# The order of values, denominators and key/value products in a fused gated attention and expert kernel

## The chip, the cores and the metric

The kernel runs on one core of one Trainium2 chip. Its time is the device time of one launch in microseconds (us). The core has TensorE (PE in the rows; PEld are its weight loads), VectorE (DVE), ScalarE (ACT), GpSimd (POOL) and SyncE (SP, which issues the transfers). They run their own instruction streams in order and meet through semaphores.

## What is computed

The reference is a gated cross attention followed by a gated layer of experts, in float32:

```python
x = x + tanh(g_xattn) * xattn(layernorm(x), ctx)        # x: 4 x 512 x 256, ctx: 4 x 1024 x 256
x = x + tanh(g_ffn) * ffn(layernorm(x))

# xattn, 16 heads of 64
lat, ctx = layer_norm(latents), layer_norm(context)
q = lat @ Wq                                            # 256 -> 1024
k, v = split(ctx @ Wkv)                                 # 256 -> 2 x 1024
k = rope(k, cos, sin)                                   # x1*cos - x2*sin, x2*cos + x1*sin
attn = softmax(clip(q k^T / 8, -11, 11))
out = (attn v) @ Wo + bo

# ffn: 4 experts of width 1024, each row goes to 2 of them, exact gelu
```

## The kernel before

**Stages.** A start (to about 45 us) loads and transposes the first batch, then the attention runs over 128 steps (to about 870 us), then come the routed experts. A batch has four units of four heads, a unit has eight steps (s = 0 to 7), and its two halves are pairs of heads (p), with c = s % 4 as the step within a pair. i = u * 8 + s counts the steps of a batch, 0 to 31. The loop over the batches in the program holds units 1, 2, 3 and the next batch's unit 0; the last three units are written out apart, with `last` true.

**One step.** It works on two context tiles of 128 rows for one pair:
- TensorE, `score`: the scores of the two tiles, twelve matmuls (L1519) into the banks `sc0` and `sc1`. Products that need float32 accuracy are made of three matmuls of a high and a low part.
- ScalarE, `exps`: exponential of each bank into `prob` (L800), 128 x 1024 each. `prob` has two halves by the step's parity.
- VectorE, `clamp`: the clip, as a clamp of the exponentials (L1004), for each bank; `sums`: adds them into `acc` (L1016 for c = 1, L1019 for c = 2 and 3; nothing for c = 0).
- TensorE, `values`: attention times values for the *preceding* step, eight matmuls into `pv` (L1533). They wait for that step's clamps (`clamped`).
- TensorE, `kv_make`: keys and values of tile s of the *next* unit, six matmuls into the bank `kv` (L1464 to L1466). They wait until VectorE has read that bank for the tile before (`rot1`).
- The key's rotation: ScalarE copies key and value out of `kv` (`kv_evac`, L748 and L749); GpSimd multiplies by the sines (L610); VectorE multiplies by the cosines from `kv` (`rot_cos`, L993); GpSimd adds the two (L614, semaphore `rot`).
- TensorE, `k_turn`: transposes the rotated key of the tile *before* this step's (L1505) into the bank `tr`. It waits for `rot` and `k_ready`. ScalarE rounds it to the high part (`k_split`, L742), VectorE makes the low part (`k_low`, L957, semaphore `k_ready`), which also frees `tr`.

**Once in a pair.** In its first step (c = 0), `denominators` (L1543, into the bank `mi`) sums `acc` of the pair before over the partitions, and waits for both last sums; VectorE then makes `reciprocals` (L1024, L1028, L1032). In the second step (c = 1) VectorE's `normalise` (L1038) reads `pv` first of all, and `values`, which begin a new accumulation in `pv` there, wait for it; `q_make` makes the next pair's query. For s = 2 and 3 `project` multiplies by the output weights and `residual` adds the product on VectorE.

**The steps that turn.** The next batch's context is normalised and transposed beside this work: for i = 18 to 25 a step ends with `ctx_turn` (L1471), for i = 26 and 27 with `lat_turn` (L1478), both into `tr`, and so both wait for `k_ready` of this step's key. ScalarE's `ctx_affine` (L758, four pieces) reads them and stands ahead of the next step's exponentials; VectorE's `ctx_low` (L943) makes their low part one step later. For i = 19 to 28 (`turned`) `kv_make` stands ahead of `k_turn`, since the bank `tr` is longer in use. In the last batch the router's rows are turned in the same way for i = 10 to 15 (`x_turn`), with `turned` for i = 11 to 16. Just ahead of the turning, GpSimd's `lat_scale` (L590 to L596) makes the latents' scale in i = 15, behind the output weights' low part (L604).

**What sets the order.** No scheduler: each engine's `step` function writes its instructions out, and the engine takes them in that order. All four `step` functions are called with the same (b, u, s). The change touches those of VectorE and of TensorE.

## Time and profile before

| | us |
|---|---|
| median of 3 runs | 1193.79 |
| lowest and highest | 1192.82 to 1195.61 |
| profiled execution | 1203.28 |
| its span, first to last instruction | 1201.5 |
| TensorE busy | 1123.1 (93%) |
| VectorE busy | 1026.8 (85%) |
| ScalarE busy | 649.5 (54%) |
| GpSimd busy | 617.9 (51%) |

The busy times are of the profiled execution. A busy TensorE is not a TensorE at its peak, since matmuls overlap and their ends are modelled: the distance from start to start of two groups tells what one costs. The TensorE clock that was granted is 0.987 of full speed over the span. In the rows a wait stands in brackets behind an instruction: the engine's idle time just before it, and what ended it.

### The profile page before, as it was taken

To read this page: it belongs to the slowest core of one execution; us is meant where nothing else is said; L and a number is where in the kernel's file an instruction comes from. 1 tells how busy PE (TensorE), PEld (TensorE's weight loads), DVE (VectorE), ACT (ScalarE), POOL (GpSimd) and SP (SyncE) were. 2 spreads that over 40 slices of the span, in tenths; PEclk is the share of its full clock that TensorE was granted. 3 is DMA by queue.
4 is the path that set the end of the run, shared out by engine and by line. 5 is a ranking of instruction groups with operands and counts; after the bars stand their busy time and mean duration, and the time that the engine had idled before them with its cause. 6 is when DMAs were issued, how large, how long until landed. Compare 5 with 4: busy or idle time off the path is not lost.

```text
span 1201.5 us, 22865 instructions
## 1 busy us (share of the span) xinstructions
PE 1123.1 (93%) x8087; PEld 758.0 (63%) x8087; DVE 1026.8 (85%) x1751; ACT 649.5 (54%) x1223; POOL 617.9 (51%) x593
## 2 busy tenths in 40 slices
PE   5799999999999999999999999997789989999987
PEld 3555555555555555465555556653379989999777
DVE  6699999898899998989999998889678777775886
ACT  4555566655456665455666455534456666663321
POOL 5333565343356535335644343238558767885750
PEclk9999999999999999999999999999999999999989
DMA  6000100000000000000000022002347555665102
GB/s 176 32 10 15 31 23 14 10 10 20 19 19 28 10 10 10 21 19 19 28 10 10 18 79 72 10 23 102 123 136 242 194 172 179 204 218 176 51 29 70
DMA packets 67080, 79.33 MB, mean 66 GB/s; under 512 B 10888, under 2 KB 60432, under 8 KB 66960
## 3 DMA queue, kind: packets, MB, share of 16 engines
q1 hardware_dynamic: 64640, 71.47, 18.5%
q0 software_dynamic: 2304, 6.29, 1.6%
q8 instruction: 70, 1.15, 0.4%
q14 instruction: 50, 0.41, 0.1%
q10 hardware_dynamic: 16, 0.00, 0.0%
HBM read 64.65 MB, written 13.11 MB: 65 GB/s over the span
## 4 chain that ended last, share of the span: by engine, by line
PE 68%; DVE 15%; POOL 6%; issue 6%; ACT 2%; DMA 1%; SPq 1%; another core or an unknown queue 0%; POOLq 0%; DVEq 0%; ACTq 0%
PE pv L1533 14%; PE sc L1519 12%; PE kv L1464 5%; PE kv L1466 4%; PE kv L1465 4%; PE sc L1464 4%; PE sc L1466 4%; PE sc L1465 4%; PE tr L1505 3%; DVE acc L1019 3%; PE mi L1464 3%; PE mi L1465 3%; PE mi L1466 3%; POOL slots_x L639 2%; PE mi L1543 2%
## 5 line engine op out<-in xcount | busy, mean ns | idle before, releaser
L800 ACT ACTIVATE prob<-sc 128x1024 f32<-128x1024 f32 x256 | 249.6, 1028 | 217.8 <-PE sc L1519 210.6
L610 POOL TENSOR_TENSOR rot_s<-k_raw,sinb 128x256 f32<-128x256 f32 x128 | 108.7, 850 | 389.3 <-ACT k_raw L748 389.3
L1533 PE MATMUL pv<-prob,val 128*32 128x512 f32 x2048 | 245.7, 597 | 3.0 <-DVE recip L1038 1.8
L1519 PE MATMUL sc<-q_hid,big 64*128 64x512 f32 x1536 | 214.7, 411 | 10.1 <-ACT prob L800 6.4
L1004 DVE TENSOR_SCALAR prob<-prob 128x1024 f32<-128x1024 f32 x256 | 183.8, 731 | 44.5 <-ACT prob L800 40.3
L1519 PEld LDWEIGHTS sc<-q_hid,big 64*128 64x128 f32 x1536 | 135.8, 186 | 115.0 <-issue 68.4
L1019 DVE TENSOR_TENSOR acc<-acc,prob 128x1024 f32<-128x1024 f32 x128 | 195.6, 1549 | 0.0
L614 POOL TENSOR_TENSOR rot_c<-rot_c,rot_s 128x256 f32<-128x256 f32 x128 | 122.0, 953 | 42.0 <-DVE rot_c L993 27.0
L1533 PEld LDWEIGHTS pv<-prob,val 128*32 128x32 f32 x2048 | 56.6, 109 | 111.9 <-issue 90.8
L1464 PE MATMUL kv<-big,acts 128*128 128x512 f32 x256 | 114.5, 447 | 6.2 <-DVE rot_c L993 5.0
L659 POOL TENSOR_TENSOR big<-prob,big 128x512 fp32r<-128x512 f32 x72 | 92.6, 1294 | 49.0 <-ACT big L827 45.2
L659 POOL TENSOR_TENSOR big<-val,big 128x512 fp32r<-128x512 f32 x72 | 93.1, 1300 | 27.6 <-ACT big L827 23.1
L1466 PE MATMUL kv<-big,acts 128*128 128x512 f32 x256 | 102.4, 400 | 0.0
L1465 PE MATMUL kv<-big,acts 128*128 128x512 f32 x256 | 102.1, 399 | 0.0
L1464 PE MATMUL sc<-big,q_hid 128*128 128x256 f32 x304 | 89.5, 295 | 10.5 <-DVE q_hid L1374 10.0
L1016 DVE TENSOR_TENSOR acc<-prob 128x1024 f32<-128x1024 f32 x64 | 93.7, 1503 | 0.0
L1465 PE MATMUL sc<-big,q_hid 128*128 128x256 f32 x304 | 87.1, 287 | 1.1 <-issue 1.1
L1466 PE MATMUL sc<-big,q_hid 128*128 128x256 f32 x304 | 87.2, 287 | 0.0
L748 ACT ACTIVATE k_raw<-kv 128x256 f32<-128x256 f32 x128 | 50.1, 391 | 62.5 <-PE kv L1466 59.9
L993 DVE TENSOR_TENSOR rot_c<-kv,cosb 128x256 f32<-128x256 f32 x128 | 53.8, 420 | 34.7 <-ACT val L749 30.5
L1464 PEld LDWEIGHTS sc<-big,q_hid 128*128 128x128 f32 x304 | 59.3, 195 | 13.5 <-DVE q_hid L1374 12.4
L1505 PE MATMUL tr<-ident,rot_c 128*128 128x128 f32 x256 | 54.3, 294 | 12.9 <-POOL rot_c L614 12.9
(250 smaller groups left out, 2515.3 us busy)
## 6 DMA issues: line engine op xcount, KB each, us to landing
val<-in_L_ffn_w SPq DMA_DIRECT2D x18, 1024.0 KB, 5.6
prob<-in_L_ffn_w SPq DMA_DIRECT2D x18, 1024.0 KB, 5.6
rows<-in_ctx SPq DMA_DIRECT2D x32, 128.0 KB, 2.1
w_raw<-in_L_xattn_Wq SPq DMA_DIRECT2D x16, 256.0 KB, 2.6
w_raw<-in_L_xattn_Wo SPq DMA_DIRECT2D x64, 64.0 KB
slots_x<-c_aff SPq DMA_DIRECT2D x1, 3840.0 KB, 13.1
rows<-slots_x SPq DMA_DIRECT2D x15, 256.0 KB, 7.9
slots_y<-acc SPq DMA_DIRECT2D x15, 256.0 KB, 2.1
```

The lines of the kernel that those rows point to most:

```text
L610: g.tensor_tensor(rot_s[:].rearrange("p (h a c) -> p h a c", h=4, a=2), kh[:, :, ::-1, :], sinb[:, t].unsqueeze(1).to_broadcast([P, 4, 2, ...
L614: g.tensor_tensor(k_rot[:], rot_c[:], rot_s[:], ALU.add).then_inc(rot, 1)
L659: low = g.tensor_tensor(w_of(job, half, 1)[:, cols], raw_of(job, half)[:, cols], w_of(job, half, 0)[:, cols].bitcast(F32), ALU.subtract)
L800: a.activation(prob[:, s % 2, i, :], sc[i][:], ACT.Exp, scale=DH ** -0.5).then_inc(exp_done[i], 1)
L1004: v.tensor_scalar(prob[:, s % 2, i, :], prob[:, s % 2, i, :], EXP_LOW, EXP_HIGH, ALU.max, ALU.min).then_inc(clamped[i], 1)
L1016: v.tensor_tensor(acc[:, i, :], prob[:, 0, i, :], prob[:, 1, i, :], ALU.add).then_inc(summed[i], 1)
L1019: v.tensor_tensor(acc[:, i, :], acc[:, i, :], prob[:, s % 2, i, :], ALU.add).then_inc(summed[i], 1)
L1464: mm(dst, lhs(0), rhs(0), start=start, stop=False, **kw)
L1465: mm(dst, lhs(0), rhs(1), start=False, stop=False, **kw)
L1466: return mm(dst, lhs(1), rhs(0), start=False, stop=stop, **kw)
L1519: last = mm(sc[i][:, h * N:(h + 1) * N], kst[rows_h, u % 2, j, lk, t * P:(t + 1) * P], q_sp[rows_h, p % 2, lq, :], start=lk + lq == 0, sto ...
L1533: last = mm(pv[g * 32:(g + 1) * 32, :], val[:, u % 2, 2 * c + i, at:at + 32], prob[:, s % 2, i, h * N:(h + 1) * N], start=c == 0 and i == ...
```

## The change

On TensorE, in every step of the attention:
- `values` of the preceding step come directly behind the scores, where c is not 1. Where c is 1 they stay last of the group, behind key transpose, key/value product, output product and query.
- `denominators` follow the values, ahead of key transpose and key/value product.
- So the key/value product ends the plain step, or is followed only by the output product. Where `turned` is true it stands ahead of the key transpose as before, and the transpose is then followed directly by the context's or the latents'.

On VectorE, the first of the two sums comes directly behind the clamps, ahead of `rot_cos` and `k_low`; the context's and the latents' low parts move ahead of it, so that they are still made before it. The second sum stays behind.

```diff
@@ VectorE, step
                 clamp(b, u, s, 1)
+                if not last and 0 <= i - TURN - 1 < ST:
+                    ctx_low(b + 1, i - TURN - 1)
+                if not last and 0 <= i - L_TURN - 1 < 2:
+                    lat_low(b + 1, i - L_TURN - 1)
+                sums(b, u, s, 0)
                 if make:
                     rot_cos(*next_unit(b, u), s)
                 if s == 0:
...
                 if last and i == R_RANK + 2:
                     route_slots()
-                if not last and 0 <= i - TURN - 1 < ST:
-                    ctx_low(b + 1, i - TURN - 1)
-                if not last and 0 <= i - L_TURN - 1 < 2:
-                    lat_low(b + 1, i - L_TURN - 1)
-                sums(b, u, s, 0)
@@ TensorE, step
                 score(b, u, s, 1)
+                if c != 1 and not (is_first(b, u) and s == 0):
+                    values(*((b, u, s - 1) if s else (b, u - 1, STEPS - 1) if u else (b - 1, UNITS - 1, STEPS - 1)))
+                if c == 0 and not (is_first(b, u) and s == 0):
+
+                    pe.wait_ge(q_ready, pair_no(b, p) + 1)
+                    wait(pe, wo_out, (b * UNITS + u) * 2 - (2 if s == 0 else 0))
+                    denominators(*((b, p - 1) if p else (b - 1, PAIRS - 1)))
                 turned = not last and 0 <= i - TURN - 1 < ST + 2 or last and R_TURN < i <= R_TURN + EH
                 if make and turned:
                     kv_make(nb, nu, s)
...
                 if make and not turned:
                     kv_make(nb, nu, s)
-                if c == 0 and not (is_first(b, u) and s == 0):
-
-                    pe.wait_ge(q_ready, pair_no(b, p) + 1)
-                    wait(pe, wo_out, (b * UNITS + u) * 2 - (2 if s == 0 else 0))
-                    denominators(*((b, p - 1) if p else (b - 1, PAIRS - 1)))
...
-                if not (is_first(b, u) and s == 0):
+                if c == 1:
                     values(*((b, u, s - 1) if s else (b, u - 1, STEPS - 1) if u else (b - 1, UNITS - 1, STEPS - 1)))
```

TensorE, from a pair's first step (its key/value product, L1464 to L1466) into its second, before. `kv`, `mi`, `pv`, `sc` and `tr` are the banks written: key/value, denominators, values, scores, key transpose.

```order
 L1465 MATMUL kv<-big,acts 128x512
 L1466 MATMUL kv<-big,acts 128x512
 L1543 MATMUL mi<-acc,ones 32x256 x8
 L1533 MATMUL pv<-prob,val 32x512 x8
 L1519 MATMUL sc<-q_hid,big 128x512 x12
 L1505 MATMUL tr<-ident,rot_c 128x128 x2
```

The same place with the change:

```order
 L1465 MATMUL kv<-big,acts 128x512
 L1466 MATMUL kv<-big,acts 128x512
 L1519 MATMUL sc<-q_hid,big 128x512 x12
 L1505 MATMUL tr<-ident,rot_c 128x128 x2
 L1464 MATMUL kv<-big,acts 128x512
```

Between a key/value product and the transpose of its key (L1505), denominators and values are gone, and the scores alone are left.

TensorE, the end of a step that turns (i = 22, c = 2), before:

```order
 L1465 MATMUL kv<-big,acts 128x512
 L1466 MATMUL kv<-big,acts 128x512
 L1505 MATMUL tr<-ident,rot_c 128x128 x2
 L1533 MATMUL pv<-prob,val 32x512 x8
 L1469 REGISTER_ALU
 L1471 MATMUL tr<-ident,rows 128x128 x2
```

and with the change:

```order
 L1465 MATMUL kv<-big,acts 128x512
 L1466 MATMUL kv<-big,acts 128x512
 L1505 MATMUL tr<-ident,rot_c 128x128 x2
 L1469 REGISTER_ALU
 L1471 MATMUL tr<-ident,rows 128x128 x2
 L1519 MATMUL sc<-q_hid,big 128x512 x12
```

The values no longer stand between the key transpose and the context transpose (L1471), which write the same bank.

VectorE, a step that turns (L1004 clamps, L943 context's low half, L1019 sums, L993 and L957 the key's rotation and low half), before:

```order
 L1004 TENSOR_SCALAR prob<-prob 128x1024
 L992 REGISTER_ALU
 L993 TENSOR_TENSOR rot_c<-kv,cosb 128x256
 L957 TENSOR_TENSOR big<-tr,big 128x2x128
 L943 TENSOR_TENSOR acts<-c_aff,acts 128x2x128
 L1018 ISA
 L1019 TENSOR_TENSOR acc<-acc,prob 128x1024 x2
```

and with the change:

```order
 L1004 TENSOR_SCALAR prob<-prob 128x1024
 L943 TENSOR_TENSOR acts<-c_aff,acts 128x2x128
 L1018 ISA
 L1019 TENSOR_TENSOR acc<-acc,prob 128x1024
 L992 REGISTER_ALU
 L993 TENSOR_TENSOR rot_c<-kv,cosb 128x256
 L957 TENSOR_TENSOR big<-tr,big 128x2x128
 L1019 TENSOR_TENSOR acc<-acc,prob 128x1024
```

The context's low half and one sum have moved ahead of the key's rotation and of its low half, which frees the bank `tr`.

## Rows read from the trace of the kernel before

**Rows 1.** Busy times, 75 to 760 us: PE, PEld, DVE, ACT, POOL, clock, DMA
```profile
75.00:760.00 685.00, 673.38 (x4835) 385.73 (x4834) 630.79 (x1046) 391.51 (x737) 309.41 (x310) 1.00 0.07 22
```

**Rows 2.** In order of time, a bare step on TensorE (start, length, engine, line)
```profile
646.86 1.67 PE L1519 MATMUL sc<-q_hid,big 64*128 64x512 f32 x12
...
648.46 0.44 PE L1505 MATMUL tr<-ident,rot_c 128*128 128x128 f32 x2
...
650.22 1.92 PE L1533 MATMUL pv<-prob,val 128*32 128x512 f32 x16
...
652.08 1.65 PE L1519 MATMUL sc<-q_hid,big 64*128 64x512 f32 x12
```

**Rows 3.** In order of time, TensorE, VectorE and GpSimd, the attention's first step
```profile
44.74 0.40 PE L1466 MATMUL kv<-big,acts 128*128 128x512 f32 x1
...
45.29 1.67 PE L1519 MATMUL sc<-q_hid,big 64*128 64x512 f32 x12
...
45.94 0.42 DVE L993 TENSOR_TENSOR rot_c<-kv,cosb 128x256 f32<-128x256 f32 x1 [2.24 <-ACT val L749]
...
46.28 0.41 DVE L957 TENSOR_TENSOR big<-tr,big 128x256 fp32r<-128x256 f32 x1
...
46.88 0.72 POOL L614 TENSOR_TENSOR rot_c<-rot_c,rot_s 128x256 f32<-128x256 f32 x1 [0.51 <-POOL rot_s L610]
...
47.66 0.44 PE L1505 MATMUL tr<-ident,rot_c 128*128 128x128 f32 x2 [0.70 <-POOL rot_c L614]
```

**Rows 4.** In order of time, TensorE alone, context transposes of one batch
```profile
572.81 0.44 PE L1471 MATMUL tr<-ident,rows 128*128 128x128 f32 x2
...
593.35 0.44 PE L1471 MATMUL tr<-ident,rows 128*128 128x128 f32 x2
...
599.17 0.43 PE L1471 MATMUL tr<-ident,rows 128*128 128x128 f32 x2
...
605.41 0.43 PE L1471 MATMUL tr<-ident,rows 128*128 128x128 f32 x2 [0.56 <-DVE big L957]
...
612.28 0.43 PE L1471 MATMUL tr<-ident,rows 128*128 128x128 f32 x2 [0.33 <-DVE big L957]
...
619.29 0.44 PE L1471 MATMUL tr<-ident,rows 128*128 128x128 f32 x2
```

**Rows 5.** In order of time, ScalarE and TensorE, the step from 605.77 us
```profile
606.13 0.81 ACT L758 ACTIVATE acts<-tr,affine 128x128 fp32r<-128x128 f32 x2 [1.82 <-DVE acts L943]
...
607.51 1.94 ACT L800 ACTIVATE prob<-sc 128x1024 f32<-128x1024 f32 x2
...
609.17 1.07 PE L1543 MATMUL mi<-acc,ones 128*32 128x256 f32 x16
...
610.05 1.90 PE L1533 MATMUL pv<-prob,val 128*32 128x512 f32 x16
```

**Rows 6.** In order of time, GpSimd and TensorE, step i = 17 of a batch
```profile
552.23 2.28 POOL L604 TENSOR_TENSOR wo<-w_raw,wo 128x512 fp32r<-128x512 f32 x1
...
560.92 0.44 PE L1505 MATMUL tr<-ident,rot_c 128*128 128x128 f32 x2 [1.24 <-POOL rot_c L614]
```

**Rows 7.** In order of time, TensorE and VectorE, a pair's reciprocals
```profile
663.35 1.66 PE L1519 MATMUL sc<-q_hid,big 64*128 64x512 f32 x12
...
663.57 0.43 DVE L1024 STREAM_TRANSPOSE recip<-mi 128x256 f32<-128x256 f32 x1
...
664.04 0.83 DVE L1028 RECIPROCAL rc<-recip 64x8 f32<-64x8 f32 x4
...
664.91 0.71 DVE L1032 STREAM_TRANSPOSE recip<-rc 128x512 f32<-128x512 f32 x1
```

**Rows 8.** Groups by line (busy us, mean ns of one, idle before them)
```profile
L1019 DVE TENSOR_TENSOR acc<-acc,prob 128x1024 f32<-128x1024 f32 x128 | 195.6, 1549 | 0.0
...
L1004 DVE TENSOR_SCALAR prob<-prob 128x1024 f32<-128x1024 f32 x256 | 183.8, 731 | 44.5 <-ACT prob L800 40.3 <-issue 0.8 <-DVE gate L1302 0.2
```

**Rows 9.** In order of time, GpSimd, a rotation beside a softmax sum
```profile
656.96 1.76 POOL L614 TENSOR_TENSOR rot_c<-rot_c,rot_s 128x256 f32<-128x256 f32 x1
```

## The prediction

> **What bounds the kernel now.** I read four views in this order. First the busy time by stretches: between 75 and 760 us, where the attention runs at full pace, TensorE is busy 673.38 of 685 us at a granted clock of 1.00 and VectorE 630.79 us [rows 1]. So TensorE sets the time there, with 11.6 us of idle time in all, and VectorE is close behind. Second the instructions in order of time in a bare step (one with no denominators, no query or output product): scores, key transpose, key/value product and values follow each other without a hole. From 646.86 to 652.08 that is 5.22 us: 1.60 for the scores (to 648.46), 1.76 for transpose and product (to 650.22), 1.86 for the values [rows 2]. Third the same view of TensorE's context transposes (L1471), whose distances give the lengths of the steps that also turn the next batch's context [rows 4]. Fourth the waits with VectorE at the end of them in those steps [rows 5]. Since TensorE is nearly full, whatever makes it wait anew adds to the time, and a gain can't exceed those 11.6 us by much: I look for what each new place in the order waits for.
>
> The Trainium skill (Perfetto Trace Analysis, Identifying the Most-Contended Engine) says that matmul busy time is no good measure of how near TensorE is to its limit, and to look at the weight loads, here 385.73 of 685 us [rows 1]. By that one would see room on TensorE, and the sum below would shrink towards nothing. The start-to-start distances of a bare step, without a gap between groups [rows 2], decide against it.
>
> **Part 1, the order on TensorE in plain steps.** The products are the same; only who stands behind whom changes. Before, a key/value product was followed by values (1.86) and scores (1.60) before its key was transposed. Now, where c is not 1, it is followed by scores and values: the same 3.46 us, so the rotation on ScalarE, GpSimd and VectorE stays hidden. Costed at nothing. In a pair's second step (c = 1) only the scores stand between: 1.60 us. What the rotation needs, the start of the attention shows, where no values exist yet and the order is exactly this one: the product's last matmul starts at 44.74 and ends at 45.14, VectorE's half starts at 45.94, GpSimd's sum at 46.88, the transpose at 47.66, after 0.70 us of idle TensorE [rows 3]. That wait is the least the order can cost with the engines otherwise idle; I take 0.65, as an estimate that lets the two engines overlap slightly better than there (bounds 0.55, and 0.9 for a VectorE that is late). Steps of this kind with a key/value product ahead, not turning, and not already in this order: 22. That is 14.3 us.
>
> **Part 2, the same place behind GpSimd's long chain.** In step i = 17 of each of the first three batches the transpose already waits 1.24 us, because GpSimd works from 552.23 on the output weights and the latents' scale before it can rotate; the transpose comes at 560.92 [rows 6], 8.69 us later. The chain starts when the rotation of step i = 15 is done, and that step's product now stands behind the values instead of ahead of them, 1.86 us later. The chain and the transpose behind it slip by about 1.9 us; 0.65 is counted already, so 1.25 more, three times: 3.8 us (bounds 0 and 6).
>
> **Part 3, the denominators.** They stay about 3.4 us into a pair's first step, now behind the values. They wait for the last sum. VectorE reaches the pair's second step later: in the first step its rotation waits for a product that is now last, so the transposes and reciprocals (0.43 + 0.83 + 0.71, from 663.57 to 665.62 [rows 7]) start when the key's low half is written, some 1.5 us after the step's end, where 663.57 was 0.2 us behind the end at 663.35. That is 1.3 us later at VectorE, against 0.7 us by which the next pair's denominators come later (0.65 of part 1 and 0.1 of order). Only where bare steps leave VectorE little slack (a unit's end, 10 times) can the rest surface: 0.4 us each, 4 us; bounds 0 and 1.2 each.
>
> **Part 4, the steps that turn.** Ten steps of each of the first three batches (i = 19 to 28) put the key/value product ahead of the key transpose, and nine end with a context or latent transpose into the same bank. It must wait until VectorE has read the key out of that bank. Before, the values (1.86) stood between and covered this. Now only c = 1 keeps them there. After a product's end the key's low half is written 1.55 us later at best (46.28 + 0.41 against 45.14 [rows 3]). And VectorE now does its first sum (mean 1.549 us [rows 8]) between the clamps and the rotation, which closes a loop: context transpose 0.43, ScalarE starts 0.05 later, its four affine pieces 1.4 (606.13 to 607.51), two exponentials 1.94, last clamp 0.73, context's low half 0.34, first sum 1.55, rotation 0.34 and key's low half 0.41, and again the transpose: 7.26 us [rows 5, 8]. (0.34 is the start-to-start distance of two such operations in rows 3.)
> - A pair's last step: 7.26.
> - A pair's first step has no sum, but scores 1.60, values 1.86, denominators 0.88 (609.17 to 610.05), product 1.6 and 1.6 for rotation and low half, with 0.4 for the transpose: 7.9.
> - Second step: the reciprocals and normalisation (0.43 + 0.83 + 0.71 [rows 7], and the product with `pv`) take longer than ScalarE's part of the loop; an estimate of 0.25: 7.5.
> - Third step: the query's rounding stands ahead of the exponentials; I estimate it at 0.6, between an affine piece of 0.35 and an exponential of 0.97 [rows 5]: 7.85.
>
> Now against what rows 4 give: i = 19 to 21 took 20.54 together and become 7.26 + 7.9 + 7.5 = 22.66 (+2.1); i = 22, 5.82 to 7.85 (+2.0); i = 23, 6.24 to 7.26 (+1.0); i = 24, 6.87 to 7.9 (+1.0); i = 25, 7.01 to 7.5 (+0.5). For i = 26 and 27, which have an output product behind the key transpose and so more cover, I take half of what i = 22 and 23 lose, +1.5 together. That is 8.1 a batch, 24.3 for three. The lower bound leaves the loop out and keeps only the 1.6 us behind the product in steps without an output product: 4 a batch, 12. The upper takes GpSimd beside VectorE, below: 12 a batch, 36.
>
> In the last batch six steps turn the router's rows in the same manner, with fewer waits behind them; I take 2 us in all, bounds 0 and 5. Later steps of that batch wait for routing work that nothing here moves: nothing.
>
> **GpSimd beside VectorE.** A rotation sum takes 0.72 us alone [rows 3] and 1.76 us beside a softmax sum [rows 9]. The first sum now lies where GpSimd multiplies k by the sines. In plain steps there are 3.46 us of cover, against the 2.5 of rows 3, so 1.0 more is just hidden; I take nothing for it, and put it in the upper bounds. The Trainium skill (SBUF — State Buffer, Who interferes with whom) says that a VectorE instruction with two SBUF inputs and a GpSimd instruction that reads SBUF exclude each other for a whole instruction. The 1.76 us agrees. By that rule both of GpSimd's operations would stand behind a sum, and the third rival below would be the case; the sum here does not lean on it.
>
> **Sum.** 14.3 + 3.8 + 4 + 24.3 + 2 = 48.4 us. The profiled execution took 1203.28 us, with a span of 1201.5, so it would become 1251.7. The median of the runs without a profile is 1193.79, 9.5 us less; I add the same 48.4 to it: **1242.2 us**. By the lower bounds: 12.1 + 0 + 0 + 12 + 0 = 24; by the upper: 20 + 6 + 12 + 36 + 5 = 79.
>
> **The rivals.**
> - *The turning steps stay covered.* VectorE and ScalarE start each step earlier than I think, since the values no longer stand before the transposes, and the loop hides; only parts 1 to 3 remain: 1193.8 + 22 = 1216. For it: VectorE waits little in those steps now (0.33 us at 612.28 is TensorE's wait for it, not the reverse [rows 4]). Against: the 1.6 us behind the product need no busy VectorE.
> - *Faster.* The sum fills the hole in which VectorE waits for the value copy, so it keeps ahead of TensorE, and the 11.6 us of idle go in part: VectorE's lateness ends the idle time in front of the context transposes (0.56 and 0.33 us [rows 4]). It decides if the key's rotation fits behind the scores, that is in under 1.60 us from the product's end; then parts 1 and 4 vanish and about 8 us are gained: 1186. Against it: rows 3 show 2.5 us.
> - *GpSimd falls behind in every step.* Each key transpose of the other steps waits too, by 0.4 us in about 70 steps (the 1.0 us more of rows 9 on two operations, less the cover): 28 on top, 1270.
> - *The order doesn't bite.* Semaphores other than the order set the pace, and the time stays: 1194. Against: the order on TensorE is fixed in the program, and the engine is full.
>
> **How the numbers follow.** Forecast 0.64; turning steps covered 0.14; GpSimd behind 0.12; faster 0.07; unchanged 0.03. The range leaves out the faster and the unchanged case and the far end of the third: 1212 to 1272. A measurement of this kernel can tell about 0.2% (2.4 us) from no change. Faster by more 0.07, within 0.03, slower 0.90.
>
> **What would show it.** Right: TensorE's key transposes (L1505) wait for GpSimd's L614 in every second step of a pair, by 0.55 to 0.9 us; its context transposes (L1471) wait for VectorE's L957 by 1 to 2 us; a bare plain step stays at 5.2 us; the idle time between 75 us and the attention's end grows from 11.6 to about 58 us; the expert stage behind it keeps its length. Wrong, and how: if L1471 shows no new wait, part 4 falls; if L1505 waits in steps with c = 2 and 3 too, the third rival holds; if the denominators (L1543) wait over 1 us, part 3 was too small.

## The result, and the profile with the change

The changed kernel takes 1248.64 us, median of 4 runs (1247.43 to 1251.06), against 1193.3 us for the kernel before (4 runs, 1191.22 to 1195.61). The ratio is 1.0471, with a 95% interval of 1.0446 to 1.0497. It is slower by 55.3 us. The prediction was 1242.2, within 1212 to 1272.

The profiled execution took 1247.43 us, with a span of 1245.7. The attention of the last batch now ends some 55 us later, so I read 75 to 815 us where [rows 1] have 75 to 760. The columns are those of [rows 1]:

```profile
75.00:815.00 740.00, 685.62 (x4868) 392.94 (x4864) 622.82 (x1057) 396.79 (x743) 292.92 (x314) 0.99 0.07 20
```

TensorE is idle for 54.4 us (740.00 - 685.62) where it was idle for 11.6. The mean clock fell from 1.00 to 0.99, which looks like nothing and is not. The two longest sums of waits in the same stretch, TensorE only (sum in us, how often, longest):

```profile
PE tr L1505 <- POOL rot_c L614: 24.8, 23, 2.8
PE tr L1471 <- DVE big L957: 19.6, 21, 1.6
```

Before, the same two stood at 6.6 and 2.6 us over 75 to 815 us (4.1 and 2.6 over 75 to 760 us, which holds about the same steps):

```profile
PE tr L1505 <- POOL rot_c L614: 6.6, 6, 1.5
...
PE tr L1471 <- DVE big L957: 2.6, 6, 0.6
```

Two kinds of wait were foreseen and both came. Where they lie is seen best by the length of each step, from the start of its scores (L1519) to the start of the next one's. Subtracting the two kernels step by step, up to step 124 of 128, gives 54.99 us, nearly the 55.3 us of the medians. A second profile of the kernel before, below, is 2.7 us later at that step, so this is known to about 3 us. By kind of step (us, the changed kernel minus the kernel before, from one profile of each):

| steps | how many | predicted | measured |
|---|---|---|---|
| plain second steps, c = 1 | 17 | 0.65 each | +9.6, 0.56 each |
| i = 17 | 3 | 1.9 each | +9.3, 3.1 each |
| i = 15 | 3 | 0 | +7.1, 2.4 each |
| turning, i = 19 to 27 | 27 | +24.3 | +18.8 |
| the last batch, i = 8 to 16, with its turning steps | 9 | +2 | +5.2 |
| all other steps up to there | 54 | +4 | +1.3 |
| start, and the attention's end | 11 | 0 | +3.7 |

The first row holds one step that had the changed order already (the attention's second) and kept its length. The other 16 lost 0.60 us each. A 17th of this kind, i = 9 of the last batch (+0.6), is in the fifth row, together with i = 8 (-0.8, at the end of the program's loop); i = 10 to 16 alone are +5.3.

**A plain second step** (i = 13 of the second batch), TensorE, VectorE and GpSimd in order of time. The product's last matmul is followed by the scores alone, and the transpose waits 0.57 us. The rotation's pieces are those of [rows 3], at nearly the same distances:

```profile
346.38 0.40 PE L1466 MATMUL kv<-big,acts 128*128 128x512 f32 x1
346.70 1.66 PE L1519 MATMUL sc<-q_hid,big 64*128 64x512 f32 x12
...
347.27 0.74 POOL L610 TENSOR_TENSOR rot_s<-k_raw,sinb 128x256 f32<-128x256 f32 x1 [4.63 <-ACT k_raw L748]
...
347.50 0.43 DVE L993 TENSOR_TENSOR rot_c<-kv,cosb 128x256 f32<-128x256 f32 x1 [1.95 <-ACT val L749]
...
348.15 0.73 POOL L614 TENSOR_TENSOR rot_c<-rot_c,rot_s 128x256 f32<-128x256 f32 x1
...
348.94 0.44 PE L1505 MATMUL tr<-ident,rot_c 128*128 128x128 f32 x2 [0.57 <-POOL rot_c L614]
```

**A turning step** (i = 22 of the third batch). It now lasts from 634.33 to 641.61, 7.28 us, where it lasted 5.8. The last product matmul ends at 639.44, VectorE's first sum stands ahead of the rotation, and the context transpose waits 1.59 us for the key's low half:

```profile
639.05 0.39 PE L1466 MATMUL kv<-big,acts 128*128 128x512 f32 x1
639.24 1.22 DVE L1019 TENSOR_TENSOR acc<-acc,prob 128x1024 f32<-128x1024 f32 x1
...
640.38 0.42 DVE L993 TENSOR_TENSOR rot_c<-kv,cosb 128x256 f32<-128x256 f32 x1
640.71 0.41 DVE L957 TENSOR_TENSOR big<-tr,big 128x256 fp32r<-128x256 f32 x1
641.04 1.21 DVE L1019 TENSOR_TENSOR acc<-acc,prob 128x1024 f32<-128x1024 f32 x1
...
641.25 0.43 PE L1471 MATMUL tr<-ident,rows 128*128 128x128 f32 x2 [1.59 <-DVE big L957]
641.61 1.20 PE L1519 MATMUL sc<-q_hid,big 64*128 64x512 f32 x8
```

**Step i = 15** was a bare step of 5.20 us and now takes 7.57, in all three batches. I had not foreseen this one. VectorE and GpSimd, with the transpose that waits:

```profile
581.68 1.20 DVE L1019 TENSOR_TENSOR acc<-acc,prob 128x1024 f32<-128x1024 f32 x1
581.83 3.97 POOL L614 TENSOR_TENSOR rot_c<-rot_c,rot_s 128x256 f32<-128x256 f32 x1
...
582.81 1.28 DVE L1004 TENSOR_SCALAR prob<-prob 128x1024 f32<-128x1024 f32 x2
584.01 1.21 DVE L1019 TENSOR_TENSOR acc<-acc,prob 128x1024 f32<-128x1024 f32 x1
...
585.86 0.44 PE L1505 MATMUL tr<-ident,rot_c 128*128 128x128 f32 x2 [2.31 <-POOL rot_c L614]
```

GpSimd's addition, 0.72 us alone [rows 3] and 1.76 us beside one sum [rows 9], takes 3.97 us. It starts 0.15 us behind the start of one sum and ends (585.80) 0.58 us behind the end of the next (585.22). VectorE runs sum, clamp, clamp, sum there, four instructions without a gap.

**Step i = 17** waits as in [rows 6], but 2.78 instead of 1.24 us, and then something else happens:

```profile
590.86 1.75 POOL L604 TENSOR_TENSOR wo<-w_raw,wo 128x512 fp32r<-128x512 f32 x1
...
598.13 0.44 PE L1505 MATMUL tr<-ident,rot_c 128*128 128x128 f32 x2 [2.78 <-POOL rot_c L614]
...
598.64 0.39 PE L1465 MATMUL kv<-big,acts 128*128 128x512 f32 x1
...
599.59 0.63 PE L1465 MATMUL kv<-big,acts 128*128 128x512 f32 x1
```

The same matmul goes from 0.39 to 0.63 us. TensorE and its clock in two stretches there (us, TensorE busy, granted clock, transfers' share and rate):

```profile
600.00:602.50 2.50, 2.50 (x7) 0.51 0.01 3
602.80:604.60 1.80, 1.80 (x17) 1.00 0.00 0
```

After the wait the clock was granted at the lower of its two levels (1.2 GHz) for some 3 us, and step i = 17 is longer by 1.54 us of wait and about 1.56 us of slow matmuls.

### The profile page after: what moved, and what is told of

Read it like the earlier page. It is cut to its first block, busy times and chain, and to the rows that moved or that the text cites. A ratio compares the mean times of both kernels' runs of the same rounds, so it can differ in the third digit from the quotient of the medians.

```text
span 1245.7 us, 22865 instructions
## 1 busy us (share of the span) xinstructions
PE 1128.9 (91%) x8087; PEld 759.3 (61%) x8087; DVE 1001.3 (80%) x1751; ACT 652.6 (52%) x1223; POOL 599.7 (48%) x593
## 4 chain that ended last, share of the span: by engine, by line
PE 61%; DVE 16%; issue 8%; POOL 8%; ACT 6%; DMA 1%; SPq 0%; POOLq 0%; DVEq 0%; ACTq 0%
PE pv L1533 13%; PE sc L1519 9%; PE kv L1464 5%; PE kv L1466 4%; PE kv L1465 4%; PE sc L1464 4%; PE sc L1466 4%; PE sc L1465 4%; PE tr L1505 2%; POOL rot_c L614 2%; DVE acc L1016 2%; ACT prob L800 2%; POOL rot_s L610 2%; POOL slots_x L639 2%; PE mi L1543 2%
## 5 line engine op out<-in xcount | busy, mean ns | idle before, releaser
L610 POOL TENSOR_TENSOR rot_s<-k_raw,sinb 128x256 f32<-128x256 f32 x128 | 112.2, 877 | 437.0 <-ACT k_raw L748 436.9
L1533 PE MATMUL pv<-prob,val 128*32 128x512 f32 x2048 | 248.3, 603 | 4.2 <-DVE recip L1038 3.0
L1004 DVE TENSOR_SCALAR prob<-prob 128x1024 f32<-128x1024 f32 x256 | 193.7, 773 | 51.7 <-ACT prob L800 49.0
L1519 PE MATMUL sc<-q_hid,big 64*128 64x512 f32 x1536 | 217.3, 415 | 13.9 <-ACT prob L800 8.9
L1519 PEld LDWEIGHTS sc<-q_hid,big 64*128 64x128 f32 x1536 | 138.0, 188 | 84.1 <-issue 59.4
L1019 DVE TENSOR_TENSOR acc<-acc,prob 128x1024 f32<-128x1024 f32 x128 | 170.9, 1336 | 0.0
L614 POOL TENSOR_TENSOR rot_c<-rot_c,rot_s 128x256 f32<-128x256 f32 x128 | 125.6, 981 | 69.9 <-DVE rot_c L993 55.9
L1533 PEld LDWEIGHTS pv<-prob,val 128*32 128x32 f32 x2048 | 53.7, 110 | 129.3 <-issue 123.3
L993 DVE TENSOR_TENSOR rot_c<-kv,cosb 128x256 f32<-128x256 f32 x128 | 53.7, 419 | 97.3 <-ACT val L749 85.2
L1464 PE MATMUL kv<-big,acts 128*128 128x512 f32 x256 | 115.2, 450 | 7.0 <-DVE rot_c L993 5.7
L1466 PE MATMUL kv<-big,acts 128*128 128x512 f32 x256 | 103.7, 405 | 0.0
L1464 PE MATMUL sc<-big,q_hid 128*128 128x256 f32 x304 | 89.3, 294 | 11.0 <-DVE q_hid L1374 10.8
L1466 PE MATMUL sc<-big,q_hid 128*128 128x256 f32 x304 | 86.8, 285 | 0.0
L1505 PEld LDWEIGHTS tr<-ident,rot_c 128*128 128x128 f32 x256 | 29.4, 144 | 91.7 <-POOL rot_c L614 51.5
L1505 PE MATMUL tr<-ident,rot_c 128*128 128x128 f32 x256 | 54.5, 295 | 31.6 <-POOL rot_c L614 31.5
```

Source lines behind the costliest of these rows:

```text
L610: g.tensor_tensor(rot_s[:].rearrange("p (h a c) -> p h a c", h=4, a=2), kh[:, :, ::-1, :], sinb[:, t].unsqueeze(1).to_broadcast([P, 4, 2, ...
L614: g.tensor_tensor(k_rot[:], rot_c[:], rot_s[:], ALU.add).then_inc(rot, 1)
L1004: v.tensor_scalar(prob[:, s % 2, i, :], prob[:, s % 2, i, :], EXP_LOW, EXP_HIGH, ALU.max, ALU.min).then_inc(clamped[i], 1)
L1019: v.tensor_tensor(acc[:, i, :], acc[:, i, :], prob[:, s % 2, i, :], ALU.add).then_inc(summed[i], 1)
L1464: mm(dst, lhs(0), rhs(0), start=start, stop=False, **kw)
L1466: return mm(dst, lhs(1), rhs(0), start=False, stop=stop, **kw)
```

## The experiments

The experiments ran on three chips. The kernel before took 1192.23 us (7 runs), 1204.98 us (11) and 1193.02 us (17) on them, so ratios are compared, each with the runs of before on its own chip. Diffs are against the changed kernel unless said otherwise. Lengths of steps come from the profiled execution and scatter less than the medians.

**How much is scatter.** The kernel before again, nothing changed.

> The kernel before, unchanged, for a second profile. The changed kernel's steps are 55 us longer by the 125th step (901.31 against 846.32 us), but its profiled execution is only 44 us longer than that of before, so the stage behind was 11 us shorter there. If that is an accident of before's one profile, in which the granted clock was 0.93 from 1100 us on, this profile has the same step lengths to 0.1 us and a span near 1192 us. If the changed order really shortens the stage behind, the span is again near 1201 us.

It took 1190.98 us. Its steps have the lengths of the first profile within 0.05 us, but for two kinds: those around the seam of the program's loop (i = 7 and 8; +2.2 us in the second and third batch, -0.5 in the last), and the attention's end, +1.2. By step 124 it is 2.7 us later than in the first profile. So the +1.3 and most of the +3.7 us of the table's last rows are not told apart from scatter. The 1.5 us of it that i = 8 of the third batch takes more are the clock: i = 8 takes 7.6 us where the granted clock is 0.50 behind the wait at the seam (second batch in both profiles, third in the second) and 6.07 where it stays at 1.00. The span was 1189.2 against 1201.5, all of it behind the attention. There the first profile had a granted clock of 0.95 over its last 141 us, and this one 0.99 over its last 129:

```profile
1060.00:1201.00 141.00, 126.21 (x823) 115.40 (x821) 101.72 (x140) 45.96 (x80) 71.37 (x61) 0.95 0.31 103
```
```profile
1060.00:1189.00 129.00, 120.97 (x827) 111.31 (x825) 91.05 (x141) 46.44 (x81) 71.63 (x61) 0.99 0.34 113
```

From step 124 to the end it is 355.2 us in the first profile, 340.2 in the second and 344.4 with the change: what lies behind the attention shows no effect of the change that could be told from this scatter. The 9.5 us between profiled execution and median that the prediction set aside were an accident of that one execution.

### Each engine's part alone

`e1_dve_only` has VectorE's new order and TensorE's old one:

```diff
-                if c != 1 and not (is_first(b, u) and s == 0):
-                    values(...)
-                if c == 0 and not (is_first(b, u) and s == 0):
...
-                    denominators(...)
...
+                if c == 0 and not (is_first(b, u) and s == 0):
...
+                    denominators(...)
...
-                if c == 1:
+                if not (is_first(b, u) and s == 0):
                     values(...)
```

`e2_pe_only` has it the other way round:

```diff
                 clamp(b, u, s, 1)
-                if not last and 0 <= i - TURN - 1 < ST:
-                    ctx_low(b + 1, i - TURN - 1)
-                if not last and 0 <= i - L_TURN - 1 < 2:
-                    lat_low(b + 1, i - L_TURN - 1)
-                sums(b, u, s, 0)
...
                     route_slots()
+                if not last and 0 <= i - TURN - 1 < ST:
+                    ctx_low(b + 1, i - TURN - 1)
+                if not last and 0 <= i - L_TURN - 1 < 2:
+                    lat_low(b + 1, i - L_TURN - 1)
+                sums(b, u, s, 0)
```

> Only VectorE's part of the change: the first sum (and the low parts) ahead of the rotation; TensorE's order as before. Theory (what counts is what stands between a product and the transpose that waits for it on TensorE): the old order keeps 3.46 us of cover, so most plain steps keep their length; only steps that already wait for VectorE get longer by the 1.2 us of a sum (i = 23, 24 and perhaps 20, 22), with some waits of GpSimd: 1200 to 1212 us. Rival (VectorE's order makes most of the loss, since the key's rotation comes a sum later everywhere): over 1225 us.

> Only TensorE's part: values and denominators behind the scores, VectorE's order as before. Theory: the waits of the key transposes in c = 1 (0.57 us each) and of the context transposes (1.4 to 1.6 us) stay to within 0.2 us, since they follow from what stands behind the product; the two sums now both come behind a late rotation, so the denominators wait 0.5 to 1 us in a pair's first step: 1250 to 1270 us. Rival (the first sum ahead of the rotation makes the waits): the waits of the context transposes fall under 0.5 us and the time is below 1225 us.

Measured: VectorE's part alone 1211.79 us, ratio 1.0164 (1.0128 to 1.0200); TensorE's part alone 1242.39 us, ratio 1.0409 (1.0368 to 1.0449). The first fell at the upper end of its expectation, the second 8 us under the lower end of its own. By kind of step, against the kernel before (us; the columns from e3 on are of experiments further down, each by the first letters of its name):

| steps | both | VectorE | TensorE | e3 | e4 | e6 | e7 | e9 |
|---|---|---|---|---|---|---|---|---|
| plain c = 1 | +9.6 | -0.5 | +12.0 | +8.3 | +6.6 | +9.6 | +8.3 | +6.0 |
| i = 17 | +9.3 | -1.0 | +0.1 | +8.9 | 0.0 | +5.5 | +9.0 | +0.5 |
| i = 15 | +7.1 | +1.6 | 0.0 | +8.5 | 0.0 | 0.0 | +8.5 | 0.0 |
| turning | +18.8 | +18.3 | +15.4 | +16.6 | +18.7 | +18.8 | 0.0 | 0.0 |
| last batch, i = 8 to 16 | +5.2 | -0.8 | +7.4 | +0.4 | +4.8 | +3.6 | +0.5 | 0.0 |
| others but seam, start, end | 0.0 | +2.6 | +13.3 | -0.3 | +0.5 | 0.0 | -0.2 | +0.3 |

- In the turning steps either part alone costs nearly what both cost, in sum. The two mechanisms of part 4 (the product now behind the values, and the sum ahead of the rotation) run side by side and don't add up. Which of them counts changes from step to step, and at i = 22 both parts together cost less than VectorE's alone (see the table by step further down).
- With TensorE's part alone the steps with denominators wait, for the last sums. From the waits of 75 to 815 us in that kernel (sum, how often, longest):

```profile
PE mi L1543 <- DVE acc L1019: 15.2, 16, 1.6
```

That is what part 3 of the prediction describes. With VectorE's part added it is gone: the sum that stands ahead of the rotation fills the time in which VectorE would wait for the product.
- Of the +7.1 at i = 15 and the +9.3 at i = 17, one part alone gives 1.6 at most. They need both.

### The turning steps: which of two limits

`e3_turn_old` gives TensorE its old order where `turned` is true, with VectorE's new order kept. It tells the product path from the loop through VectorE's sum.

```diff
+                late = c == 1 or turned
-                if c != 1 and not (is_first(b, u) and s == 0):
+                if not late and not (is_first(b, u) and s == 0):
                     values(...)
-                if c == 0 and not (is_first(b, u) and s == 0):
+                if c == 0 and not late and not (is_first(b, u) and s == 0):
...
+                if c == 0 and late:
+                    denominators(...)
...
-                if c == 1:
+                if late:
                     values(...)
```

> The changed kernel, but in the steps that turn (the flag turned) values and denominators stand where they stood before; VectorE's order stays changed. Theory: the values cover the 1.55 us behind the product again, so i = 19 to 27 lose most of their +6.3 us a batch and the last batch's turning steps theirs: about 24 us less than the changed kernel, 1222 to 1230. Rival (the loop through ScalarE and VectorE with a sum in it, as in part 4 of the prediction): these steps stay at 7.1 to 7.3 us where they are bare, and the time is above 1238.

It took 1235.06 us, ratio 1.0356 (1.0325 to 1.0388), and the turning steps keep +16.6 of +18.8 us. The time lies between the two that were expected; the lengths of the steps speak for the rival, with 7.34 us for i = 23. The loop is real. The same step as above, i = 22 of the third batch, with values between product and context transpose:

```profile
637.12 0.69 DVE L1004 TENSOR_SCALAR prob<-prob 128x1024 f32<-128x1024 f32 x1
...
637.44 0.96 POOL L610 TENSOR_TENSOR rot_s<-k_raw,sinb 128x256 f32<-128x256 f32 x1 [2.21 <-ACT k_raw L748]
...
637.73 0.96 DVE L943 TENSOR_TENSOR acts<-c_aff,acts 128x256 fp32r<-128x256 f32 x1
...
638.61 1.21 DVE L1019 TENSOR_TENSOR acc<-acc,prob 128x1024 f32<-128x1024 f32 x1
...
639.74 0.41 DVE L993 TENSOR_TENSOR rot_c<-kv,cosb 128x256 f32<-128x256 f32 x1
640.08 0.41 DVE L957 TENSOR_TENSOR big<-tr,big 128x256 fp32r<-128x256 f32 x1
...
640.62 0.43 PE L1471 MATMUL tr<-ident,rows 128*128 128x128 f32 x2 [2.14 <-DVE big L957]
```

The chain has no gap: clamp, the context's low half (slowed to 0.96 us by GpSimd beside it), first sum, rotation, low half, transpose. The last batch's turning steps lose their 5.2 us to 0.4, so there the order on TensorE was the whole cause.

`e7_turn_both_old` goes one step further and puts back VectorE's order in the turning steps too; the plain steps keep the new order on both engines. The diff beyond that of `e3_turn_old`:

```diff
                 clamp(b, u, s, 1)
-                if not last and 0 <= i - TURN - 1 < ST:
-                    ctx_low(b + 1, i - TURN - 1)
-                if not last and 0 <= i - L_TURN - 1 < 2:
-                    lat_low(b + 1, i - L_TURN - 1)
-                sums(b, u, s, 0)
+                turning = not last and TURN < i <= TURN + ST + 2 or last and R_TURN < i <= R_TURN + EH
+                if not turning:
+                    sums(b, u, s, 0)
...
+                if not last and 0 <= i - TURN - 1 < ST:
+                    ctx_low(b + 1, i - TURN - 1)
+                if not last and 0 <= i - L_TURN - 1 < 2:
+                    lat_low(b + 1, i - L_TURN - 1)
+                if turning:
+                    sums(b, u, s, 0)
```

> The changed kernel, but in the steps that turn both TensorE's and VectorE's order are as before. Alone, the old order on TensorE left these steps at +16.6 us, the old order on VectorE at +15.4. Theory (two limits of nearly the same length lie on these steps, the 1.55 us behind the product and the loop with a sum in it; each must go): the 27 turning steps lose at least 17 of their 18.8 us and the last batch's return to before, so 1223 to 1229 us. Rival (something third, such as a VectorE that is late from the plain steps, holds them): more than 8 us of the 18.8 stay.

It took 1232.27 us, ratio 1.0232 (1.0191 to 1.0273), on a chip on which the kernel before took 12 us more than on the one for which 1223 to 1229 us were expected. All 18.8 us of the turning steps are gone, every one of the nine back to its length of before within 0.03 us. Here the rotation stands directly behind the clamp, and the transpose follows it without a wait (TensorE's lines are 4 higher in this kernel):

```profile
627.70 0.42 DVE L993 TENSOR_TENSOR rot_c<-kv,cosb 128x256 f32<-128x256 f32 x1
628.04 0.41 DVE L957 TENSOR_TENSOR big<-tr,big 128x256 fp32r<-128x256 f32 x1
628.37 0.42 DVE L943 TENSOR_TENSOR acts<-c_aff,acts 128x256 fp32r<-128x256 f32 x1
...
628.58 0.43 PE L1475 MATMUL tr<-ident,rows 128*128 128x128 f32 x2
```

### The plain second step: more cover

`e4_q_first` puts the query product directly behind the scores in plain second steps, so that it lies between a product and its transpose.

```diff
                 turned = ...
+                if c == 1 and not turned and not (last and p == PAIRS - 1):
+
+                    wait(pe, den_turned, pair_no(b, p))
+                    q_make(*next_pair(b, p))
...
-                if c == 1 and not (last and p == PAIRS - 1):
+                if c == 1 and turned and not (last and p == PAIRS - 1):
```

> The changed kernel, but in c = 1 (where the flag turned is not set) the query product stands directly behind the scores, ahead of the key transpose. Theory: the 1.4 us of the query are cover for the key's rotation, so no key transpose of c = 1 waits for GpSimd except at i = 17; but the query itself must wait for the first transpose of the reciprocals, about 0.35 us. Net 0.25 us less in each of 17 plain second steps and about 1.4 us less at each of three i = 17: 1239 to 1244 us, against 1248.6 for the changed kernel. Rival (the wait belongs to the key transpose's own chain, whatever stands ahead of it): key transposes still wait 0.5 us or more and the time stays within 2 us of the changed kernel's.

It took 1237.7 us, ratio 1.0288 (1.0244 to 1.0331). The transpose's wait goes, but the query product waits for VectorE's transpose of the denominators, with which it shares the bank `mi`:

```profile
338.06 0.44 DVE L1024 STREAM_TRANSPOSE recip<-mi 128x256 f32<-128x256 f32 x1
338.63 0.50 PE L1464 MATMUL mi<-acts,wq 128*128 128x512 f32 x1 [0.38 <-DVE recip L1024]
```

So second steps gain only 3 of 9.6 us, 0.6 of it in the attention's second step, which the change had left as it was. The larger gain is at i = 15 and i = 17, which are back to their lengths of before, 16.4 us; at i = 17 the expectation had 1.4 us for each, at i = 15 nothing. In the step i = 15 GpSimd's addition now starts closer behind VectorE's sum:

```profile
564.91 1.22 DVE L1019 TENSOR_TENSOR acc<-acc,prob 128x1024 f32<-128x1024 f32 x1
564.98 1.73 POOL L614 TENSOR_TENSOR rot_c<-rot_c,rot_s 128x256 f32<-128x256 f32 x1
566.04 1.82 DVE L1004 TENSOR_SCALAR prob<-prob 128x1024 f32<-128x1024 f32 x2
```

`e5_before_q` makes the same move, with the same lines, in the kernel before.

> The kernel before with the same move of the query product ahead of the key transpose in c = 1. Theory: it covers the 1.24 us at the three steps i = 17 and the 0.4 us in steps 9 and 10 of the first batch, and costs nothing, since VectorE's reciprocals come earlier there: 4 to 5 us less than before, a ratio of 0.996. Rival: the query waits for the reciprocals in other steps too and takes the gain back: ratio 1.000 or more.

It took 1227.01 us, ratio 1.0199 (1.0160 to 1.0238): 2% slower where I expected a slight gain. The wait at i = 17 went as expected (-3.7 us), but steps with denominators wait for the last sums, and third steps with an output product for the query's low half (L999), which now comes later against them:

```profile
357.56 0.64 PE L1543 MATMUL mi<-acc,ones 128*32 128x256 f32 x8 [0.85 <-DVE acc L1019]
```
```profile
371.26 0.38 PE L1464 MATMUL mi<-wo,acts 128*128 128x256 f32 x1 [1.36 <-DVE q_hid L999]
```

Steps outside the kinds of the table's first rows lose 16.6 us. In the old order VectorE has no room for the move; the sum ahead of the rotation is what makes it.

### Steps 15 and 17: GpSimd's addition beside VectorE

Theory: GpSimd's addition gets through only when VectorE pauses. Rival: it is late because the chain ahead of it on GpSimd is. At i = 15 VectorE also makes statistics of the latents (L964, L967), 0.4 and 0.2 us a step. `e6_stats_early` moves these two steps earlier in the batch and touches nothing else.

```diff
-        L_AGG, L_NORM = SCALE - NT - 1, SCALE
+        L_AGG, L_NORM = SCALE - NT - 3, SCALE
```

> The changed kernel with the latents' statistics on VectorE two steps earlier (i = 8 to 12 in place of i = 10 to 14); nothing else. At i = 15 the changed kernel's key transpose waits 2.31 us for a GpSimd addition that took 3.97 us while VectorE ran without a gap. Theory (GpSimd gets through only in a gap of VectorE, and the statistics of i = 13 and 14 close the last gap in two bare steps): the addition falls under 2 us and the three steps i = 15 go back to 5.2 us, 7 us less, about 1242. Rival (the addition is slow because a sum runs beside it, gap or no gap): the wait at i = 15 stays above 1.5 us.

It took 1250.36 us, ratio 1.0383 (1.0341 to 1.0425), from 1.0471. The step i = 15 is back at 5.20 us in all three batches:

```profile
574.26 0.42 DVE L993 TENSOR_TENSOR rot_c<-kv,cosb 128x256 f32<-128x256 f32 x1 [0.24 <-ACT val L749]
...
574.92 0.73 POOL L614 TENSOR_TENSOR rot_c<-rot_c,rot_s 128x256 f32<-128x256 f32 x1
574.94 1.79 DVE L1019 TENSOR_TENSOR acc<-acc,prob 128x1024 f32<-128x1024 f32 x1
```

VectorE now has a pause of 0.24 us ahead of the rotation and has finished its sum of the step before. GpSimd's addition starts 0.02 us ahead of the sum, takes 0.73 us, and it is the sum that is longer. In the changed kernel the sum started 0.15 us ahead of the addition, and the addition took 3.97.

So the repair works, but the theory as I had put it is not borne out. The addition doesn't need a pause to run in: here it runs beside the key's low half and the sum, which follow each other without one, and in `e4_q_first` it takes 1.73 us beside sum, clamp, clamp, sum without a gap. What the traces show is that the start counts. In the changed kernel, between 45 and 760 us, additions that start at least 0.03 us ahead of a sum take 0.73 us, and the sum 1.6 to 1.8. Those that start 0.03 to 0.17 us behind the start of a sum take 1.6 to 1.8 us where something other than a clamp follows it, and 3.97 us in the one place where clamps and another sum follow (i = 15). With 0.07 to 0.09 us behind, in `e4_q_first`, the same clamps follow and it takes 1.7 us. By what rule GpSimd gets its turn among the clamps the traces don't show, so the cause of the full 3.97 us stays open.

The rival (late because the chain ahead of it is) explains the start only: counted from the step's scores, GpSimd's multiplication ends 0.36 us earlier here, since it no longer lies beside a sum (0.74 us instead of 1.07), and that is enough to put the addition ahead of the sum.

Step i = 17 gained 3.8 us, and its three instances tell why: 9.25, 9.23 and 10.67 us. In the first two the transpose waits 2.60 us and the clock stays; in the third it waits 2.77 us and the clock falls, as in all three of the changed kernel. The length of the wait doesn't decide it: in `e3_turn_old` the clock falls behind waits of 2.60 us too, and behind one of three waits of 2.31 us at i = 15. Granted clock over 2 us after each (the columns of [rows 1]):

```profile
372.00:374.00 2.00, 2.00 (x13) 1.40 (x15) 2.00 (x5) 1.38 (x5) 1.00 (x2) 1.00 0.01 4
```
```profile
589.00:591.00 2.00, 1.83 (x6) 1.54 (x7) 2.00 (x5) 0.00 (x0) 1.43 (x3) 0.50 0.03 8
```

Without the clock's fall the step costs 1.36 us more than before, all of it wait (2.60 against 1.24).

`e8_before_stats` makes the same edit in the kernel before, in the hope of a version that beats it.

> The kernel before, with VectorE's statistics of the latents two steps earlier in a batch (i = 11 to 14 region instead of up to i = 16). Theory: GpSimd's two-input additions need a gap in VectorE's stream. In the kernel before the only key transpose that waits for GpSimd is that of i = 17, 1.24 us in each of three batches; with the statistics gone from i = 15 and 16, GpSimd's chain ends earlier and that wait shrinks or goes: 0 to 3.7 us less, ratio 0.997 to 1.000. Step i = 15 itself keeps its 5.20 us, since it never waited here. Rival: the wait at i = 17 is the chain's own length and VectorE has no part in it; then i = 17 stays at 7.88 us and the ratio is 1.000, or 1.000 to 1.003 where the statistics delay a clamp in the step that they move to.

It took 1191.98 us (12 runs), ratio 0.9993 (0.9976 to 1.0011): no difference that can be told. Step i = 17 is at 7.88 us as before, and its wait is the same 1.24:

```profile
348.75 2.28 POOL L604 TENSOR_TENSOR wo<-w_raw,wo 128x512 fp32r<-128x512 f32 x1
...
357.43 0.44 PE L1505 MATMUL tr<-ident,rot_c 128*128 128x128 f32 x2 [1.24 <-POOL rot_c L614]
```

From L604 to the transpose it is 8.68 us, as in [rows 6]. In the kernel before, that wait is the chain's own length and VectorE's statistics have no part in it: here the rival was right.

### All repairs together

`e9_all_mended` is the changed kernel with the three diffs of `e7_turn_both_old` (and so of `e3_turn_old`), `e4_q_first` and `e6_stats_early`.

> The changed kernel with all four repairs that single runs tried: both engines' old order in the turning steps, the query product directly behind the scores in plain second steps, statistics two steps earlier. Theory (every loss is a wait of its own place): turning steps, i = 15, i = 17 and the last batch's turning steps come back to their lengths of before (-18.8, -7.1, -9.3, -4.7), second steps keep +6 to +7 of +9.6 us, the loop's seam +1 to +4 and the start +1: 8 to 12 us above the kernel before, ratio 1.007 to 1.010. Rival: the repairs get in each other's way, as the query product did in the order of before, where it cost 20 us in steps with denominators and output product: ratio above 1.015.

It took 1202.54 us, ratio 1.0088 (1.0065 to 1.0111). The steps sum up to 7.8 us above the kernel before, of which 6.0 in the plain second steps; the rest of the table's kinds are within 0.5 us. That is as expected, and the ratio too. Nearly every loss in the table was a wait of its own place, with or without a fall of the clock behind it, and could be taken away there. What stays is the second step: its transpose has too little behind the product, and what can be put there waits itself. No version beat the kernel before.

## Why the prediction was right, and where it was not

**What bounds it.** Right. TensorE was full, the new waits reached the end, and the 55.0 us counted on TensorE are close to the 55.3 us of the medians. The rule of the Trainium skill on this (Perfetto Trace Analysis, Identifying the Most-Contended Engine: go by the share of the peak arithmetic rate and by the weight loads, not by matmul busy time) would, by its second measure, have promised room, with 385.73 of 685 us [rows 1]. There was none.

**Part 1, second steps.** Right: 0.60 us a step (0.4 to 0.75) against 0.65 taken, since the rotation's pieces did keep nearly the distances of [rows 3]. Steps with c = 2 and 3 lose nothing but at i = 15 (and 0.1 us at i = 31), and the bare step is at 5.20 us as before. But "costed at nothing" for those steps counted the cover of 3.46 us against a rotation of 2.5 and 1.0 us more, and at i = 15 the addition alone took 3.25 us more than its 0.72.

**Part 2, i = 17.** The mechanism was right. The wait grew by 1.54 us where 1.9 was taken. The chain slipped by more than that (it starts 3.24 us behind the start of step i = 16, before 0.29 us), but took less, 7.27 us to the transpose (590.86 to 598.13) against 8.69, with 1.75 us instead of 2.28 for L604. What failed is that a wait was priced at its length. This one brought the clock down and cost as much again: 3.1 us.

**Part 3, denominators.** Wrong, 4 us taken and nothing measured. The step that failed: "VectorE reaches the pair's second step later". It held the old order of VectorE against the new one of TensorE. `e2_pe_only` shows this wait, 15.2 us of it; the first sum ahead of the rotation removes it. The two halves of the change belong together here, which I had not seen.

**Part 4, turning steps.** The mechanism was right, the size 24.3 against 18.8. By step:

| i | 19 to 21 | 22 | 23 | 24 | 25 | 26, 27 |
|---|---|---|---|---|---|---|
| predicted | +2.1 | +2.0 | +1.0 | +1.0 | +0.5 | +1.5 |
| measured | +1.85 | +1.5 | +0.8 | +1.1 | +0.3 | +0.7 |
| VectorE's part alone (third batch) | +0.75 | +2.0 | +1.1 | -0.4 | +0.3 | +1.8 |
| TensorE's part alone (third batch) | +1.5 | +1.3 | +0.8 | +1.2 | 0.0 | +0.1 |

The pair's first step came out at 7.94 us against 7.9: it goes by the product path, which has no estimate in it. The mis-sized term is the first sum. I took the mean of all sums, 1.549 us [rows 8]. In the mean are sums slowed by GpSimd beside them, and the first sum took 1.20 to 1.22. The prediction's own addition is off too: its terms give 7.19 us, not 7.26. With 1.21 for 1.55 the loop is 6.85 us, shorter than scores, values, product, 1.55 and transpose: 1.60 + 1.86 + 1.6 + 1.55 + 0.43 = 7.04, and a pair's last step (i = 23) measured 7.08. So the product path bound i = 20, 23 and 24, where TensorE's part alone loses about as much as both. The other steps it did not bind: at i = 21 and 25 TensorE's part alone loses nothing and VectorE's as much as both, and at i = 22 the rows shown further up have VectorE's sum directly ahead of the rotation, without a wait, so that the loop set its 7.28 us. For i = 22 the term of 0.6 for the query's rounding was a little long as well.

In `e3_turn_old`, where only the loop is left, the same steps take 7.34 (i = 23), 7.82 (i = 22) and 7.35 us (i = 25), near the 7.26, 7.85 and 7.5 of the prediction. That is luck in part: the sum is shorter there too, but GpSimd's multiplication falls beside the context's low half and makes it 0.96 us. In the changed kernel it comes later in i = 22 and 23 and the low half takes 0.42. This is why both parts together cost less there than VectorE's alone. `e7_turn_both_old` shows that nothing third holds these steps. Half of the loss for i = 26 and 27 was too much.

**The last batch** lost 5.2 us instead of 2, by the same product path: 0.4 remain with TensorE's old order. The term had no working behind it. About 1.5 us of it are slow matmuls again, in one step, i = 15 (scores of 2.50 us instead of 1.66), here behind a wait of only 1.05 us:

```profile
806.15 0.63 PE L1564 MATMUL tr<-ident,rows 128*128 128x128 f32 x4 [1.05 <-DVE big L957]
806.71 2.50 PE L1519 MATMUL sc<-q_hid,big 64*128 64x512 f32 x12
```

**GpSimd beside VectorE.** The sum held nothing for it, and 7.1 us came from it at i = 15. I had the two rows, 0.72 and 1.76 us, and read the second as the worst case. At i = 15 the addition stayed behind four VectorE instructions and took 3.97. The Trainium skill (SBUF — State Buffer, Who interferes with whom) says that the port pair which VectorE and GpSimd share is an exclusive lock; that the first to issue keeps it for the whole instruction and the other is fully blocked it says of VectorE's two-port modes. The 1.76 us agrees, and so does the other order (addition 0.73 us, sum 1.79). But the rule speaks of one instruction, and the 3.97 us needs the loser to lose again at each next one, which it did not do in `e4_q_first`.

**In sum**, 55.0 us in the steps against 48.4. Second steps and i = 17 together are 18.9 against 18.1 (three of the 22 steps that the 18.1 are for lie in other rows), the clock's 4.7 (3 x 1.56) making up for shorter waits. Too little: i = 15 by 7.1, the last batch by 3.2, seam, start and end by 5.0 (scatter for the most part). Too much: turning steps by 5.5, denominators by 4. The forecast was near partly because these cancel. Of the rivals, *turning steps covered* and *faster* fell by the rows that they were to be judged by, and *GpSimd behind in every step* came true in one step of a batch's 32 only.

## What to carry to other kernels

Where an engine is full, write down for each producer what now stands between it and its consumer, and compare that with the shortest chain seen in a stretch where nothing else runs; that gave 0.65 us for waits of 0.57. Take a duration from the instance that will stand there, with the same neighbours, not from a group's mean over slowed and free ones. Two new limits on the same step don't add, and two new orders on two engines may repair each other: test each half alone. Where GpSimd works beside VectorE's sums, look at which of the two starts first and at what follows the sum; 0.2 us in the start made 3.2 us in the duration here.

## What was not expected of the hardware

- A GpSimd addition of two tensors, 0.72 us alone, took 3.97 us while VectorE ran sum, clamp, clamp, sum without a gap, and ended only behind them. It had started 0.15 us behind the first sum. 0.07 us behind it, with the same four instructions and no gap, it took 1.73 us, and the first clamp 1.23 instead of 0.68. When it started 0.02 us ahead of the sum it took 0.73, and the sum 1.79 instead of 1.21. With TensorE's part alone it took 3.72 to 3.73 us at i = 21 of all three batches, beside two sums.
- TensorE's granted clock was 0.51 in the stretch behind a wait of 2.78 us, and full behind waits of 2.31 and 2.60. But it was 0.50 behind a wait of 2.31 us (i = 15 of the second batch in `e3_turn_old` and `e7_turn_both_old`), behind one of 1.87 at the seam in the kernel before, and full behind one of 2.63 at the seam of the changed kernel. The wait's length alone doesn't tell. The price was 1.3 to 1.6 us for about 3 us at the lower level. A window of 740 us shows it as 0.99 against 1.00.
- Between two profiles of one kernel the seam of the program's loop scatters by 2 us, the attention's end by 1 and what lies behind the attention by 15; all other steps repeat within 0.05 us.
